# A cross-attention kernel: earlier Wk load, four reordered places in its first and last batch, and a final sum that adds bias and residual first

## What is computed

```python
query, keyt, valt = hidden @ Wq, enc @ Wk, enc @ Wv
hs = mha(query, keyt, valt)                      # main attention, 718 keys
ca_q1 = einsum('btc,th->bch', ca, Wq_ca)[:, indices]   # 100 of 384 rows
ca_hs1 = mha(ca_q1, hidden, hidden)
ca_hs2 = mha(ca_hs1 @ Wq, ca @ Wk_ca, ca @ Wv_ca)      # 4 keys
out = (hs + ca_hs2) @ Wout + b_out + hidden
```

## Time and profile before

| what | us |
|---|---|
| median of 3 runs | 985.36 (984.73 to 988.87) |
| the profiled execution, its own time | 982.17 |
| its span (first to last instruction of the core) | 980.5 |
| PE busy | 962.7 (98%) |
| DVE / ACT / POOL busy | 708.7 / 491.8 / 343.5 |
| DMA queue of SP, share of 16 engines | 75.4% |

### The profile page before, as it was taken

The page is one execution under the profiler, slowest core; times in us unless marked ns, Lnnn a source line. Parts: engine busy times, 40 slices in busy tenths (PEclk is TensorE's granted clock), DMA queues, the critical chain, the costliest instruction groups (busy, mean ns, idle before and its releaser), DMA issues.

```text
span 980.5 us, 21024 instructions
## 1 busy us (share of the span) xinstructions
PE 962.7 (98%) x6644; PEld 942.8 (96%) x6644; DVE 708.7 (72%) x1257; ACT 491.8 (50%) x911; POOL 343.5 (35%) x302
## 2 busy tenths in 40 slices
PE   9999989999999999999999999999999999998998
PEld 8998889999999999999999999999999999998997
DVE  6455687777777778787777877777777777777444
ACT  6434545455555546464646363736464545455110
POOL 5223353434342516161615252433433433424000
PEclk9999999999999999999999999999999999999999
DMA  7899967797979787978797979787887878795364
GB/s 264 267 294 267 291 158 209 179 212 175 210 178 203 185 200 187 191 192 193 198 186 199 189 196 183 209 188 200 184 212 166 223 168 212 177 226 156 102 193 141
DMA packets 157545, 195.21 MB, mean 199 GB/s; under 512 B 81040, under 2 KB 111568, under 8 KB 157520
## 3 DMA queue, kind: packets, MB, share of 16 engines
q1 hardware_dynamic: 150000, 181.53, 75.4%
q10 hardware_dynamic: 7520, 13.35, 4.5%
HBM read 82.74 MB, written 19.95 MB: 105 GB/s over the span
## 4 chain that ended last, share of the span: by engine, by line
PE 87%; DVE 5%; DMA 4%; ACT 2%; SPq 1%; issue 0%; ACTq 0%
PE psS L780 22%; PE psB L815 17%; PE psB L820 9%; PE psS L755 8%; PE psT L796 6%; PE psS L930 6%; PE psT L848 4%; PE psT L854 2%; PE psB L825 2%; PE psB L827 2%; DMA g_split<-PT_l 1%; PE psB L880 1%; PE psB L903 1%; PE psT L855 1%; PE psB L965 1%; DVE probs L1599 1%
## 5 line engine op out<-in xcount | busy, mean ns | idle before, releaser
L780 PE MATMUL psS<-encT_keep,Wk_keep 128*128 128x360 f32 x1440 | 254.1, 330 | 0.0
L780 PEld LDWEIGHTS psS<-encT_keep,Wk_keep 128*128 128x128 f32 x1440 | 237.8, 189 | 0.7
L1172 ACT ACTIVATE probs<-psS,negmax 100x718 f32<-100x718 f32 x128 | 110.2, 861 | 132.7 <-DVE negmax L1588 132.6
L815 PE MATMUL psB<-PT_h,encN_h 128*128 128x400 f32 x480 | 169.5, 353 | 0.0
L815 PE MATMUL psB<-PT_l,encN_h 128*128 128x400 f32 x480 | 165.7, 345 | 0.0
L635 POOL TENSOR_TENSOR encT_keep<-encT_raw,encT_keep 128x718 fp32r<-128x718 f32 x45 | 83.5, 1856 | 170.1 <-ACT encT_keep L1201 165.5
L1605 DVE TENSOR_TENSOR PT_l<-psT,PT_h 128x600 fp32r<-128x600 f32 x128 | 99.5, 777 | 38.3 <-ACT PT_h L1183 35.0
L626 POOL TENSOR_TENSOR Mbd<-Mbd,fmask 128x320 fp32r<-128x320 f32 x48 | 43.1, 898 | 220.1 <-DMA Mbd<-m_split 217.5
L1588 DVE TENSOR_REDUCE negmax<-psS 100x1 f32<-100x720 f32 x128 | 114.6, 895 | 0.1
L1599 DVE TENSOR_SCALAR probs<-probs,inv 100x718 f32<-100x718 f32 x128 | 106.6, 833 | 4.5
L1183 ACT ACTIVATE PT_h<-psT 128x600 fp32r<-128x600 f32 x128 | 85.7, 669 | 44.8 <-PE psT L796 42.4
(11 more groups left out here) (253 smaller groups left out, 1791.9 us busy)
## 6 DMA issues: line engine op xcount, KB each, us to landing
kstack<-kT SPq DMA_DIRECT2D x64, 448.8 KB
kstack<-kT SPq DMA_DIRECT2D x192, 112.2 KB
enc_raw<-in_encN_dram SPq DMA_DIRECT2D x48, 384.0 KB, 4.6
encT_raw<-in_encT_dram SPq DMA_DIRECT2D x45, 359.0 KB, 5.1
kstack<-kT SPq DMA_DIRECT2D x32, 359.0 KB
kstack<-kT SPq DMA_DIRECT2D x32, 269.2 KB
kstack<-kT SPq DMA_DIRECT2D x32, 179.5 KB, 3.6
kstack<-kT SPq DMA_DIRECT2D x64, 89.8 KB, 3.9
```

The source lines that it names most:

```text
L780: mm = pe.matmul(keys_in(f, first)[:, half, 0:HALF], w[:, c, f * 128:(f + 1) * 128], e[:, c, k0:k0 + HALF], start=(j == 0), stop=(j == 3 * ...
L815: pe.matmul(psB[:, 1, 0:RH], eN[0][:, k, cc], PT[p][:, k, rows], start=(k == 0 and p == 0), stop=False)
L1172: nc.scalar.activation(halves(P[h % PRING][0:S, 0:KEYS]), without_overlap(psS[score_slot[h]], S), ACT.Exp, bias=negmax[:, h:h + 1], accum_ ...
```

## The change

- SP, prologue: the load of Wk stands ahead of group 0's q stores (its wait, wlo at 4, is unchanged and comes earlier), and store_g(0) stands behind load_heads(3, 3).
- DVE, prologue: the k2 sum stands ahead of the two v2 low parts.
- Batch 0: PE runs query(3, 4) behind turn(0, 3) and scores(0, 5); ACT runs expo(0, 5) ahead of q_high(3, 4), and DVE rowmax(0, 5) ahead of norm(0, 4). ACT runs wv_high(0) and wv_high(1) behind b2_pt2_high and wv_high(2) behind k_high(1, 2).
- Batch 15: ACT's high(0, 0) stands ahead of b2_exp2, and DVE's low(0, 0) ahead of b2_norm2.
- finish adds bias and residual first (both in SBUF) and the accumulator second. PE and ACT's stores now both follow the second addition (cres; csum guards only the first against the second). The last tile's accumulator is added, and stored, in two halves of 320 columns, and its matmuls signal each half.

```diff
--- before.py
+++ after.py
@@ -459,13 +459,13 @@
                 sp.dma_start(wvca_raw, tiled(Wvca)).then_inc(s["wvcain"], 16)
                 sp.wait_ge(s["wlo"], 3)
                 load_heads(0, 3)
+                sp.wait_ge(s["wlo"], 4)
+                sp.dma_start(wk_raw, tiled(Wk)).then_inc(s["wkin"], 16)
                 store_q(0, 0, 3)
                 store_q(0, 3, FT)
-                store_g(0)
-                sp.wait_ge(s["wlo"], 4)
-                sp.dma_start(wk_raw, tiled(Wk)).then_inc(s["wkin"], 16)
                 sp.wait_ge(s["hlo"], 3)
                 load_heads(3, 3)
+                store_g(0)
                 sp.wait_ge(s["v2lo"], 2)
                 for p in range(2):
                     sp.dma_start(raw(v2_d[p].rearrange("b t n -> (b t) n")), raw(v2st[p])).then_inc(s["v2st"], 16)
@@ -922,7 +922,7 @@
                         pe.wait_ge(s["wolo"], FT)
                         pe.wait_ge(s["exp"], HEADS * B)
                     else:
-                        pe.wait_ge(s["csum"], 2 * r + j - 1)
+                        pe.wait_ge(s["cres"], 2 * r + j - 1)
                     for half in range(2):
                         k = 0
                         for c in range(FT):
@@ -930,7 +930,8 @@
                                 mm = pe.matmul(psS[j][0:n, half, 0:HW], a[:, c, 0:n], w[:, c, half * HW:(half + 1) * HW],
                                                start=(k == 0), stop=(k == 3 * FT - 1))
                                 k += 1
-                    mm.then_inc(s["cmm"], 1)
+                        if half == 1 or n < 128:
+                            mm.then_inc(s["cmm"], 1)
 
                 def query_g(g):
 
@@ -1068,12 +1069,12 @@
                     if first:
                         query(3, 3)
                     b2_turn(i, 1)
-                    if first:
-                        query(3, 4)
-                    else:
+                    if not first:
                         context(i - 1, 5)
                     turn(i, 3)
                     scores(i, 5)
+                    if first:
+                        query(3, 4)
                     b2_xm(i)
                     if first:
                         query(3, 5)
@@ -1387,6 +1388,7 @@
                         store_q3(2)
                     b2_pt_high(i, 1)
                     if first:
+                        expo(i, 5)
                         q_high(3, 4)
                         store_q3(3)
                     else:
@@ -1396,7 +1398,6 @@
                         enc_twice(i)
                     if first:
                         xm_copy(i)
-                        expo(i, 5)
                     pt_high(i, 3)
                     if first:
                         store_q3(4)
@@ -1434,25 +1435,25 @@
                     if not last:
                         u_high(i, 0)
                     pt_high(i, 5)
-                    if first:
-                        wv_high(0)
+                    if last:
+                        high(0, 0, first=True)
                     b2_exp2(i)
                     if last:
-                        high(0, 0, first=True)
                         u_high(i, 1)
                     else:
                         k_high(i + 1, 1)
-                    if first:
-                        wv_high(1)
                     pt_high(i, 6)
                     if last:
                         high(0, 1, first=True)
                     b2_pt2_high(i)
                     if first:
-                        wv_high(2)
+                        wv_high(0)
+                        wv_high(1)
                     pt_high(i, 7)
                     if not last:
                         k_high(i + 1, 2)
+                    if first:
+                        wv_high(2)
                     if last:
                         tail_pt1(i)
                     else:
@@ -1577,8 +1578,11 @@
                 store(FULL // 2 - 1, 0)
                 load_x(FULL // 2, 0, REST)
                 store(FULL // 2 - 1, 1)
-                store(FULL // 2, 0, REST)
-                act.wait_ge(s_st[0], 16 * (FULL // 2 + 1))
+                for half in range(2):
+                    act.wait_ge(s["cres"], FULL + 1 + half)
+                    act.dma_start(out2[FULL * 128:NT, half * HW:(half + 1) * HW],
+                                  res[0][0:REST, half * HW:(half + 1) * HW]).then_inc(s_st[0], 16)
+                act.wait_ge(s_st[0], 16 * (FULL // 2 + 2))
                 act.wait_ge(s_st[1], 16 * (FULL // 2))
 
             @block.vector
@@ -1701,14 +1705,20 @@
                                             ALU.subtract).then_inc(s["clo"], 1)
 
                 def finish(r, j, n=128, first=False):
-                    dve.wait_ge(s["cmm"], 2 * r + j + 1)
                     if not first:
                         dve.wait_ge(s_st[j], 16 * r)
                     v = [halves(t[0:n, 0:H]) for t in (res[j], bias, xin[j])]
-                    nc.vector.tensor_tensor(v[0], psS[j][0:n, :, 0:HW], v[1], ALU.add).then_inc(s["csum"], 1)
+                    dve.wait_ge(s_x[j], 16 * r + 16)
+                    nc.vector.tensor_tensor(v[0], v[1], v[2], ALU.add).then_inc(s["csum"], 1)
                     dve.wait_ge(s["csum"], 2 * r + j + 1)
-                    dve.wait_ge(s_x[j], 16 * r + 16)
-                    nc.vector.tensor_tensor(v[0], v[0], v[2], ALU.add).then_inc(s["cres"], 1)
+                    if n == 128:
+                        dve.wait_ge(s["cmm"], 2 * r + j + 1)
+                        nc.vector.tensor_tensor(v[0], psS[j][0:n, :, 0:HW], v[0], ALU.add).then_inc(s["cres"], 1)
+                    else:
+                        for half in range(2):
+                            dve.wait_ge(s["cmm"], 2 * r + j + 1 + half)
+                            nc.vector.tensor_tensor(v[0][:, half, :], psS[j][0:n, half, 0:HW], v[0][:, half, :],
+                                                    ALU.add).then_inc(s["cres"], 1)
 
                 def enc0_low(c):
                     dve.wait_ge(s["enc0hi"], c + 1)
@@ -1783,13 +1793,14 @@
                     if first:
                         q_low(3, 3)
                     b2_pt_low(i, 1)
+                    if first:
+                        rowmax(i, 5)
                     norm(i, 4)
                     if first:
                         q_low(3, 4)
                     else:
                         u_low(i - 1, 5)
                     if first:
-                        rowmax(i, 5)
                         xm_add(i)
                         pt_low(i, 3)
                     else:
@@ -1820,10 +1831,11 @@
                         u_low(i, 0)
                     b2_less_max2(i)
                     pt_low(i, 5)
+                    if last:
+                        low(0, 0)
                     b2_norm2(i)
                     norm(i, 7)
                     if last:
-                        low(0, 0)
                         u_low(i, 1)
                     else:
                         k_low(i + 1, 1)
@@ -1865,15 +1877,15 @@
                 head_low(0)
                 head_low(1)
                 head_low(2)
+                dve.wait_ge(s["k2hi"], 3)
+                k2_parts = psB[0:D, :, :].rearrange("d b (h a n) -> d b h a n", h=4, a=2)
+                k2_sum4 = k2_sum.rearrange("d (b h n) -> d b h n", b=2, h=4)
+                nc.vector.tensor_tensor(k2_sum4, k2_parts[:, :, :, 0, :], k2_sum4, ALU.add).then_inc(s["k2lo"], 1)
                 for j in range(2):
                     cols = slice(j * 320, (j + 1) * 320)
                     dve.wait_ge(s["v2hi"], j + 1)
                     nc.vector.tensor_tensor(v2st[1][:, cols], psS[0][0:B * T, j, 0:320], v2st[0][:, cols],
                                             ALU.subtract).then_inc(s["v2lo"], 1)
-                dve.wait_ge(s["k2hi"], 3)
-                k2_parts = psB[0:D, :, :].rearrange("d b (h a n) -> d b h a n", h=4, a=2)
-                k2_sum4 = k2_sum.rearrange("d (b h n) -> d b h n", b=2, h=4)
-                nc.vector.tensor_tensor(k2_sum4, k2_parts[:, :, :, 0, :], k2_sum4, ALU.add).then_inc(s["k2lo"], 1)
                 dve.wait_ge(s["k2hi"], 4)
                 nc.vector.scalar_tensor_tensor(out=k2T[1].rearrange("d h n -> d (h n)"), in0=k2_sum,
                                                scalar=SCALE, in1=k2T[0].rearrange("d h n -> d (h n)"),
```

## The result

| | before | after |
|---|---|---|
| median, us | 985.36 (980.34 to 989.39, 5 runs) | 974.42 (972.86 to 976.44, 5 runs) |
| profiled execution, own time | 982.17 | 976.44 |
| its span | 980.5 | 974.7 |

The ratio of the times is 0.9895, with a 95% interval of 0.9869 to 0.992: 10.3 us less, 7.9 to 12.9 us; the two medians of the table differ by 10.9 us. The forecast was 975.8 us, a gain of 9.6 us.

The account below looks back on a forecast made before the run. PE bounds the kernel, busy 719.99 of 720 us in the loop, so only its waits outside and the end can be won: 0.5 + 1.2 + 1.4 + 0.8 + 3.0 + 1.5 + 1.2 = 9.6 us off 985.36, 975.8 us; range 973.0 to 981.0.

Parts of the forecast that it names:

- rival (d): Output stage: later residual load slows the tiles, four rounds of 2.4 us more each, 990.4 us in all; chance 0.03.
- The clock, 1.4 us: Prologue: with PE's hole filled, the clock's fall at 46 to 48 us goes; 1.4 us gained, bounds 0 and 1.4.
- rival (a): The clock falls all the same, or elsewhere in the prologue: 8.2 us gained, 977.2 us; chance 0.15.
- The Wk load, 1.2 us, and k2 ahead of v2, 0.5 us: Prologue: earlier Wk load closes PE's 1.2 us hole; k2 sum first on DVE wins 0.5 us of a 0.6 us hole.
- rival (e): Prologue: the Wk load comes no earlier in effect and PE waits as long: 7.0 us gained, 978.4 us; chance 0.05.
- So I carry all of it: Prologue to loop: the whole prologue lead of 3.1 us lasts until the loop, despite nearly full DMA.
- rival (b): Before batch 1, DMA takes back the prologue's and moved query's lead: 5.7 us gained, 979.7 us; chance 0.12.
- The query move, 0.8 us: Batch 0: turn(0, 3) and scores(0, 5) fill PE's 1.41 us wait ahead of query(3, 4); 0.8 us gained, bounds 0 and 1.2.
- wv_high, 3.0 us: Batch 0: POOL's Wv work no longer slows DVE, closing PE's waits of 1.1 and 1.9 us; 3.0 us, bounds 1.1 and 3.3.
- Rival (c): Batch 0: POOL's work only moves elsewhere, and just the first hole closes: 7.7 us gained, 977.7 us; chance 0.12.
- Batch 15, 1.5 us: Batch 15: low(0, 0) comes earlier on DVE, so PE's 1.5 us wait goes; 1.5 us gained, bounds 0.8 and 1.5.
- The end, 1.2 us: Behind the last matmul: one addition of half the columns instead of two; last store 1.2 us earlier, bounds 0.8 and 1.3.

Follow-up runs that it names:

- same_before: The kernel before, unchanged, run again against itself: ratio 0.9994 (0.9973 to 1.0014).
- prologue_alone: The kernel before with only the Wk load and store_g moved on SP and the k2 sum moved on DVE: ratio 0.998, 2.0 us gained.
- wv_moved_alone: The kernel before with only the three wv_high moved: ratio 0.9973 (0.9954 to 0.9992), 2.7 us gained.
- query_moved_alone: The kernel before with only query(3, 4), rowmax(0, 5) and expo(0, 5) moved: ratio 0.9967 (0.9948 to 0.9987), 3.3 us gained.
- after_wv_load_late: The changed kernel with the Wv load issued behind tail_pt0 and tail_enc instead of ahead: ratio 0.996 (0.9943 to 0.9978) to the kernel before.
- all_but_wv: The changed kernel with the three wv_high put back at their old places: ratio 0.9952 (0.9931 to 0.9973) to the kernel before.
- same_after: The changed kernel, unchanged, run again as a second trace: ratio 0.9921 (0.9894 to 0.9947) to the kernel before.
- pool_waits_for_p2: The kernel before with one wait added on POOL, so Wv's low parts start after ACT's b2_pt2_high: ratio 0.9967 (0.9942 to 0.9993), 3.2 us gained.
- ends_alone: The kernel before with only low(0, 0) and high(0, 0) moved in batch 15 and the new finish: ratio 0.9966 (0.995 to 0.9983), 3.4 us gained.
- all_but_prologue: The changed kernel with the four prologue moves taken back: ratio 0.9927 (0.9899 to 0.9955) to the kernel before.

## Why the prediction was right, point by point

**The sum.** 9.6 us were forecast; the two measurements of the change give 10.3 and 7.8 us (0.9895 and 0.9921). The four parts alone (prologue, query, wv_high, ends) gave 2.0, 3.3, 2.7 and 3.4 us, some 11 together, where the forecast had 3.1, 0.8, 3.0 and 2.7. The total held; of its terms only that of wv_high held both in size and in its rows. That the sum came so near is in part luck: the clock's 1.4 us rested on a wrong step, the Wk load's 1.2 us on a hole of one execution, and the query's 0.8 us doesn't show in company, while the ends gave more than their terms.

Two sums of the prediction are wrong. The upper bounds of its terms add up to 10.5 us, not 10.9, so the lower end of the range should be 973.4 us; the measured 974.42 us is inside either way. In rival (d) four rounds of 2.4 us are 9.6 us, and 10.2 us on top of the forecast would be 986.0 us; nothing there gives 990.4 us.

**The clock, 1.4 us: the step failed, rival (a) held.** "With the hole filled I expect no fall" is wrong. With the old prologue six of seven traces show a fall at 30 to 50 us, with the new one four of six, the first trace of after among them; of the three others two have theirs further on. A hole ahead of the thin products is no condition for it: in after PE's timeline has no idle time with a releaser from 27 to 52 us, and the clock falls at 33 us. The Trainium skill, "TensorE: Matmul & The Clock Gate", section "What's actually happening", has the same kernel differ from run to run; the traces agree, with some 1.5 us for a fall (4.36 against 2.82 us in after) and twice the stretch in same_before. Thirteen traces are few, but every run has its mean granted clock on record. It is 0.9955 over the 81 runs of before beside which the experiments were timed, 0.9957 over the 12 of prologue_alone, and 0.9980 over the 11 of the changed kernel. So the new prologue alone changes nothing measurable in it, and the whole change raises it. The full-speed time that went missing by these figures, (1 - clock) times the span, is 4.4 us in before and 1.9 us in after. As an estimate from them, and an upper bound, since lost clock costs nothing while PE waits, up to 2.4 us of the gain (give or take 0.8) can be clock. Which of the other moves brings that was not tested.

**The Wk load, 1.2 us, and k2 ahead of v2, 0.5 us: right in mechanism, the first too large in size.** k2's term held: the hole ahead of the first m_parts is 0.57 us in before and 0.11 us in every trace with the new prologue. The load was issued at 23.29 us instead of 29.91, and the load of heads 3 to 5 landed at 36.9 us (27.48 and 9.4 us), not at 38.5 to 39.2, so rival (e) falls. But the hole of 1.2 us was a feature of that one execution: at this place wv_moved_alone, with the old prologue and full clock, has 0.43 us, query_moved_alone 0.68 us, and the four others with the old prologue, where the clock fell earlier, none. Among traces with a fall keys(0, 0) starts at 61.5 us in the mean with the old prologue (six) and at 60.5 us with the new (four); without a fall it is 59.8 us (one) against 59.1 us (two). The two terms together are 0.8 to 1.0 us, not 1.7, by few traces and with same_before's double fall in one of the means.

**"So I carry all of it": failed in part, rival (b) in part.** In prologue_alone the whole lead of 1.6 us, and in the first trace of after 1.4 of 1.9 us, are lost between keys(0, 0) and query(3, 1), in the company of ACT's long issues of the q stores (1.92 and 1.40 us against 0.52 in before). What is left in after and the gain of the query move, 1.3 us together, is gone at pt_high(0, 4), since the g store lands at 124.1 us as in before. The load of Wv, 960 KB, is issued on SP some 4 us ahead of that store: it lands at 123.8 us in before (115.89 and 7.9) and at 123.3 us in after (114.81 and 8.5), the store 0.3 and 0.8 us behind. With the load moved behind it (after_wv_load_late) the same store lands in 2.8 us and nobody waits for it. That the load holds the store up is likely by this, but no fixed order: in all_but_wv the store lands at 122.4 us, 1.3 us ahead of the load. In same_after the load of Wv went out at 112.88 us, ACT's wait ended at 122.1 us, and 2.1 of the 3.3 us of lead were left. So the loss at the g store is real in one execution and absent in another of the same program. The step overlooked two things: that "few DMAs" on the chain is not none, and that ACT's compute stands behind the stores that ACT itself issues. That the long issues come from the nearly full DMA queues is not shown.

**The query move, 0.8 us: not settled.** 3.3 us alone, nothing measurable in company. The new wait of query(3, 5) that the text expected is there (L939, 0.5 us), and the two query waits together fell from 1.4 to 0.8 us (0.3 and 0.5).

**wv_high, 3.0 us: right.** Each row came as predicted in after: P2x 0.26 us, both holes closed, POOL behind P2x. From keys(0, 0) to turn(0, 7), the seven traces in which POOL starts behind P2x take 74.1 us in the mean, the six others 76.8 us: 2.7 us, though the two groups differ in other moves and in falls of the clock too. Even where no lead was left, from pt_high(0, 4) at 124.2 us in both, turn(0, 7) came 14.0 us later in before and 10.6 us later in after. Rival (c) falls, and pool_waits_for_p2 shows the cause. The Trainium skill, "GPSIMD Engine Reference", section "Key points", told which instructions suffer: the trace agrees, with P2x and norm's multiplication. That pt_low and k_low, which read an accumulator, don't suffer (0.77 and 0.89 us beside POOL) is what made the new place good.

**Batch 15, 1.5 us: the hole went, its time mostly not.** The wait on L930 is gone in every trace with the new ends. But from turn(0, 7) to the last sum the six traces with the old ends take 837.9 us in the mean, and the six with the new ends (the late Wv load left out) 837.6 us. In the latter stand waits on DMA, of encN_l (0.7 us in after, 1.23 in ends_alone) or of a lift (2.65 us in all_but_prologue), and some us without work within the loop. They differ from execution to execution, and some of them come with old ends too; how much of the 1.5 us they hide can't be told from these traces. The two ends together gave 3.4 us alone (1.7 to 4.9) by the medians, against the 2.7 us forecast for them, so the medians leave room for all of it.

**The end, 1.2 us: right, and too small.** 2.95 instead of 4.6 us, 1.6 us. The additions account for the 1.2 us of the forecast; the rest is the last store, which with 80 KB is done 2.5 us after its addition, where the one of 160 KB took 2.9. Rival (d) falls: the seven tiles of the last stretch take 30.76 us in both kernels, and no wait of PE on finish is listed.

## What to carry to other kernels

Where an engine's instruction is several times slower in one place than in another, look at what the other vector engine does at that moment before anything else; a wait of one line, or a later place for the work that feeds it, gave some 3 us here. Before a term is priced from one trace, ask whether it is a property of the program or of that execution: a wait of 1.2 us and a fall of the clock of 1.4 us were both of the second kind. And follow a lead to each transfer on its way, both to those whose landing someone waits for and to those that a compute engine issues itself: here three quarters of one lead went in a stretch with an issue of 1.40 us instead of 0.52, and the rest at one landing.

## What the hardware showed that was not expected

- The fall of TensorE's clock to the lower level at 30 to 50 us comes in ten of thirteen traces, at places up to 13 us apart, in after with PE busy before it (1.00 of 1.00 us in each of the two us from 31 to 33). Seven traces have falls further on, two of them two; only wv_moved_alone has none ahead of its last sum. One came at the first output tile of same_before: 6.21 us in place of the 4.67 us of before.
- norm's multiplication is slow beside other POOL instructions too: 1.64 us in before beside xTb_l (L620), 1.92 us in after beside gbd (L602), against 0.60 us alone. norm(0, 6) is slow in both kernels, and in after it lies on the chain.
- The same store of 50 KB lands in 2.8 to 5.7 us over the thirteen traces, the shortest with no large load ahead of it. ACT's issue of one q store takes 0.5 to 1.9 us in the traces compared here, and ACT's next instruction starts when it is over.
- Executions of one program differ by 4 to 10 us, in pool_waits_for_p2 by 14 us. Part of this is PE time lost inside the loop, such as 1.41 us at 300 to 500 us in ends_alone, where the other traces have 0.25 us at most, and part the clock.
